# A fused two-layer MetaFormer kernel: a strip's order of work changed, GpSimd given the FFNs' last adds, and key rows kept instead of computed again

## What is computed

```
# layer 0
x = x + conv0(ln_c(x))      # ln_c: over the 96 channels of a pixel
#   conv0: q, k, v = 1x1 convolutions; windows of 8 x 8 queries against
#   12 x 12 keys (halo 2), 6 heads of 16, relative position logits, softmax, projection
t = t + ffn0(ln_t(t))       # t: the pixels as tokens of 96
# layer 1
x = x + conv1(ln_c(x))      # per quadrant of 128 x 128 and per head of 24 (4 heads):
#   4 pooled centres, sigmoid of a cosine to each pixel, the best centre alone kept,
#   values gathered into centres, spread back to the pixels, projection
t = t + ffn1(ln_t(t))
# an FFN, with q_mul = rounding to float8 (5, 2) and q_acc to float16 (5, 10)
h = relu(q_acc(q_acc(q_mul(x) @ q_mul(W1).T) + q_mul(b1)))
y = q_acc(q_acc(q_mul(h) @ q_mul(W2).T) + q_mul(b2))
```

## Time and profile before

| | us |
|---|---|
| median of 3 runs | 9565.71 (9555.72 to 9568.57) |
| profiled execution, its own time | 9573.13 |
| its span | 9571.3 |
| TensorE busy | 8344.2 (87%) |
| TensorE weight loads busy | 6638.7 (69%) |
| VectorE busy | 7322.2 (77%) |
| ScalarE busy | 4988.4 (52%) |
| GpSimd busy | 2176.8 (23%) |
| mean granted TensorE clock | 0.905 |

### The profile page before, as it was taken

How to read it: one execution, slowest core, us unless ns; L and a number is a source line. 1 busy time by engine, 2 the same in 40 slices (tenths; PEclk the granted TensorE clock), 3 DMA queues, 4 the chain that set the end, 5 groups by cost and what they waited for, 6 DMA issues and landing times.

```text
span 9571.3 us, 441216 instructions
## 1 busy us (share of the span) xinstructions
PE 8344.2 (87%) x175538; PEld 6638.7 (69%) x175538; DVE 7322.2 (77%) x24166; ACT 4988.4 (52%) x9994; POOL 2176.8 (23%) x4356
## 2 busy tenths in 40 slices
PE   8999999998888888888888888988888989888665
PEld 6777777777767767777777766776777777776443
DVE  5777777778787777787777778777778778877666
ACT  3555445445555555555555555555555555555445
POOL 2323222222222222222222222222222222222000
PEclk9999999999999999999999999999999999998555
DMA  2111112112122122222222212222222222221111
GB/s 59 49 45 46 49 49 52 50 47 60 53 58 59 53 56 59 55 58 57 55 54 59 56 51 58 58 55 54 60 55 55 60 55 54 60 55 50 57 57 61
DMA packets 191968, 525.03 MB, mean 55 GB/s; under 512 B 33372, under 2 KB 66972, under 8 KB 189980
## 3 DMA queue, kind: packets, MB, share of 16 engines
q1 hardware_dynamic: 190204, 498.89, 19.3%
HBM read 252.61 MB, written 168.30 MB: 44 GB/s over the span
## 4 chain that ended last, share of the span: by engine, by line
PE 59%; DVE 26%; issue 8%; ACT 6%; DVEq 1%; SPq 0%; ACTq 0%; DMA 0%; POOL 0%; POOLq 0%
PE scores_x L644 10%; PE flipped L666 6%; PE bank L551 5%; PE misc L560 4%; PE pv L694 3%; PE bank L614 3%; PE bank L912 3%; DVE maxes L1510 3%; PE pv L688 3%; PE scores_x L585 2%; DVE z L1625 2%; PE bank L939 2%; PE pv L895 2%; PE bank L621 2%; DVE shifted L1518 2%
## 5 line engine op out<-in xcount | busy, mean ns | idle before, releaser
L1510 DVE TENSOR_REDUCE maxes<-scores_x 128x6 f32<-128x864 f32 x1024 | 1079.1, 1054 | 1046.3 <-PE scores_x L644 973.6
L1957 POOL TENSOR_TENSOR vrest<-vstage,vmask 96x384 f32<-96x384 f32 x512 | 431.5, 843 | 5592.6 <-ACT vstage L1141 5592.6
L644 PE MATMUL scores_x<-keys,queries 64*64 64x144 f32 x24576 | 1101.4, 313 | 436.6 <-DVE shifted L1518 414.8
L644 PEld LDWEIGHTS scores_x<-keys,queries 64*64 64x64 f32 x24576 | 803.8, 144 | 678.0 <-issue 627.9
L1179 ACT ACTIVATE probs<-flipped 128x384 f32<-128x384 f32 x1024 | 497.6, 486 | 1320.1 <-PE flipped L666 1320.1
L1518 DVE TENSOR_TENSOR shifted<-scores_x,maxes 128x768 f32<-128x768 f32 x1024 | 970.2, 948 | 0.0
L606 PE MATMUL bank<-xn,wq 97*32 97x64 f32 x24576 | 869.4, 221 | 56.7 <-issue 56.0
L666 PE MATMUL flipped<-ident,shifted 128*128 128x128 f32 x6144 | 918.6, 289 | 0.1
L603 PE MATMUL bank<-xt,wq 97*32 97x64 f32 x24576 | 846.6, 221 | 65.3 <-issue 51.0
L603 PEld LDWEIGHTS bank<-xt,wq 97*32 97x32 f32 x24576 | 727.7, 110 | 248.7 <-issue 224.8
L1129 ACT ACTIVATE queries<-bank 128x512 f32<-128x512 f32 x768 | 458.6, 597 | 835.6 <-PE bank L606 835.6
(11 more groups left out here) (185 smaller groups left out, 18387.2 us busy)
## 6 DMA issues: line engine op xcount, KB each, us to landing
x_in<-x_dram SPq DMA_DIRECT2D x128, 594.0 KB
keys<-kst SPq DMA_DIRECT2D x768, 99.0 KB
xn_kept<-xn SPq DMA_DIRECT2D x128, 388.0 KB, 3.9
later<-xn_kept SPq DMA_DIRECT2D x128, 388.0 KB, 3.3
x_tok<-tok_dram SPq DMA_DIRECT2D x128, 384.0 KB, 3.5
x_kept<-x SPq DMA_DIRECT2D x128, 384.0 KB, 2.4
later<-x_kept SPq DMA_DIRECT2D x128, 384.0 KB, 3.7
out_dram<-later SPq DMA_DIRECT2D x128, 384.0 KB, 2.5
```

Source lines behind the costliest of these rows:

```text
L644: last = mm(score[e][64 * j:64 * j + 64, g * NKEY:(g + 1) * NKEY], queries[64 * e:64 * e + 64, g, w, :], keys[64 * e:64 * e + 64, g, :, WS ...
L1510: V.tensor_reduce(maxes[:, p % 2, :, :], sc, AX.X, ALU.max).then_inc(max_ready.sem, 1)
```

## The change

In short, part by part; p numbers are pairs.

1. Only the 8 new rows of a strip are loaded, normalised and turned into keys, in 3 chunks of 352 columns (means, centring, squares, variances, spreads, key matmuls); the 4 rows shared with the strip above are copied by GpSimd (`keep_halo`) inside `xn` and `kst`. Quadrants are ordered so that a column of 32 strips runs on; at its start the top rows come by DMA (`store_tops`, `load_top`), made by two more passes of the first chain in setup.
2. Values of group 0 leave the tail and take the place of group 1 in the head; group 1 comes after the scores of pair 1, in the other banks.
3. Mixing leaves the tail: matmuls at the end of TensorE's pair 5, adds at the end of VectorE's pair 5, before the maxima of pair 6.
4. The stream's statistics: `next_stats` in pair 6, `pool_stats` in pair 7.
5. Half 1 of FFN 0's statistics and normalisation: pairs 0 and 1 of the next strip, its root in one chain with layer 1's. The flip of z of that half goes to pair 2, and so does ScalarE's copy of it. The root of the features' norm shares a chain with that of x's variance.
6. `output` and `output_c` run on GpSimd. The pooling sums its four tiles on GpSimd first, so TensorE has two matmuls.
7. All three groups of variance matmuls stand in pair 3.

```diff
@@ TensorE, attend @@
-                make_values(n, 1, work)
+                make_values(n, 0, work)
                 for p in range(TILES):
                     if p + 1 < TILES:
                         scores(p + 1)
+                    if p == 0:
+                        if on.c3:
+                            pe.wait_ge(hc_evac.sem, hc_evac.at(n - 1, 6))
+                        make_values(n, 1, fill)
...
                     if p == 3 and ahead:
-                        variance(n + 1, 2, on)
-                        variance(n + 1, 3, on)
+                        for c in range(3):
+                            variance(n + 1, c, on)
...
-                    if p == 2 and ahead:
-                        if b1:
-                            pe.wait_ge(zt_ready.sem, zt_ready.at(n - 1, 2))
-                        variance(n + 1, 0, on)
-                        variance(n + 1, 1, on)
+                    if p == 2 and b1:
+                        if on.b:
+                            pe.wait_ge(ft_ready.sem, ft_ready.at(n, 2))
+                        flip_z(n - 1, 1)
...
                     if p == 5:
                         if b2:
                             pool(n - 2)
+                        if on.c1:
+                            pe.wait_ge(v_stored.sem, v_stored.at(n, 8))
+                            mix(n, 0)
+                            mix(n, 1)
...
                 weigh(TILES - 1)
-                if on.c1:
-                    for u in range(2):
-                        if ahead:
-                            pe.wait_ge(normed.sem, normed.at(n + 1, 4 - u))
-                        pe.wait_ge(v_stored.sem, v_stored.at(n, 8))
-                        mix(n, u)
...
-                    make_main(n + 1, 0, fill)
...
-                    make_rest(n + 1, 0, fill)
@@ ScalarE, attend @@
-                    store_queries(n + 1, 5)
-                    store_rest(n + 1, 0, fill)
                 if on.c2:
                     quantise_c(n, 4)
                     quantise_c(n, 5)
+                if ahead:
+                    store_queries(n + 1, 5)
@@ VectorE, attend @@
-                    if p == 0 and on.c2:
-                        stats_c(n, 1 - par)
+                    if p == 0:
+                        if on.c2:
+                            stats_c(n, 1 - par)
+                        if b1:
+                            ffn_stats(n - 1, 1)
...
-                    if p == 1 and on.c2:
-                        rsqrt_c(n)
+                    if p == 1 and b1:
+                        ffn_normalise(n - 1, 1, False, on.c2)
...
-                    if p == 2 and on.c3:
-                        output_c(n, 0, par)
-                        output_c(n, 1, par)
...
                         normalise(0)
+                        if on.c1:
+                            mix(n, 0, par)
+                            mix(n, 1, par)
                     if p == 6:
                         if b1:
-                            dve.wait_ge(xn2_ready.sem, xn2_ready.at(n - 1, 0))
-                            if on.b2:
-                                dve.wait_ge(x2_stored, n * 16 - 16)
-                            output(n - 1, 0)
-                            output(n - 1, 1)
+                            next_stats(n - 1)
...
+                        if b1:
+                            pool_stats(n - 1)
-                if on.c1:
-                    mix(n, 0, par)
-                    mix(n, 1, par)
-                if b1:
-                    next_stats(n - 1)
                 normalise(1)
                 ffn_stats(n, 0)
-                if b1:
-                    pool_stats(n - 1)
                 ffn_normalise(n, 0, b1)
...
                 residual(1)
-                ffn_stats(n, 1)
-                ffn_normalise(n, 1, False)
@@ VectorE, drain: in lengths only the clamp is left; the chain is @@
+            def lone_root(n):
+                rsqrt(rs_b_chain, n, 128, TILES * E1, newton_d, 0,
+                      [(0, TILES * E1, rs_b_chain[3][:, 0:32], newton_n)])
@@ GpSimd @@
+            def keep_halo(n):
+                pool.wait_ge(q_ready.sem, q_ready.at(n, 6))
...
+                P.tensor_copy(xn_flat[0:PROW, 0:TOP], xn_flat[0:PROW, NEW:STRIP]
+                              ).then_inc(halo_ready.sem, 1)
+                pool.wait_ge(k_loaded, n * (16 * NH) + 16 * NH)
...
+                P.tensor_copy(kst[0:C, 0:TOP], kst[0:C, NEW:STRIP]).then_inc(halo_ready.sem, 1)
+            def output(f, u):
+                pool.wait_ge(y_evac.sem, y_evac.at(f, u + 1))
+                pool.sem_inc(gate, 1)
+                P.tensor_tensor(y16[:, u, :, :], y16[:, u, :, :],
+                                b2q[0][:, None, :].to_broadcast([128, 4, C]), ALU.add
+                                ).then_inc(y_biased.sem, 1)
+                pool.wait_ge(y_biased.sem, y_biased.at(f, u + 1))
+                pool.sem_inc(gate, 1)
+                P.tensor_tensor(x2[:, 4 * u:4 * u + 4, :], x1[:, 4 * u:4 * u + 4, :],
+                                y16[:, u, :, :], ALU.add).then_inc(x2_ready.sem, 1)
...
                 mask_values(n, 0)
                 repeat_rest(n, 2)
+                if column:
+                    take_top(column)
+                elif on.ahead:
+                    keep_halo(n)
+                mask_values(n, 1)
+                repeat_rest(n, 3)
+                if on.c3:
+                    output_c(n, 0, par)
+                    output_c(n, 1, par)
                 if on.b2:
                     normalise_stream(n - 2)
-                mask_values(n, 1)
-                repeat_rest(n, 3)
                 mask_values(n, 2)
                 mask_values(n, 3)
+                if on.b1:
...
+                    output(n - 1, 0)
+                    output(n - 1, 1)
                 if on.ahead:
                     gather(n + 1)
```

398 lines of the change are left out of this document (253 added, 145 removed).

## The result

The changed kernel takes **10089.4 us** (median of 4 runs, 10055.6 to 10169.5), the kernel before 9567.1 beside it: ratio 1.0557, 95% interval 1.0490 to 1.0625. It is 5.6% slower where 4.5% faster was forecast. The profiled execution's own time is 10110.99 (span 10109.2).

The account below looks back on a forecast made before the run. No single engine bounds it; full strips decide. Full strips 94 x -4.5, second stage -72, first -9, drain +40, setup +38 sum to -426: 9147 from 9573.1, less 7.4 gives 9140 us. Its range was 9000 to 9330; 8 in 10, 8860 to 9420.

Parts of the forecast that it names:

- Pair 5's wait: Full strips: mixing's adds delay pair 6's maxima and shift, TensorE idles 2.4 us; pair 5 in all +2.75.
- It costs: First two stages: statistics queue behind GpSimd's FFN output in pair 6, 2.2 us a first-stage strip, 3.5 a second-stage one.
- 2 late: First stage: VectorE's work in pair 1 comes 2 us late, within a forecast of -0.5 a strip.
- The clock term: Full strips: the new idle time may bring 6.8 us at half clock, at a bit over one in two: +1.9 us.
- The tail: From last attended values to scores of pair 1: 13.5 us instead of 21.86, -8.3 a full strip, the largest term.
- Pair 0: Full strips: half clock behind the idle time goes, values are added, narrower chunks help: -0.3 us; +1.65 if half clock stays.
- Pairs 1 and 2: Full strips: less mean and variance work on TensorE, -0.4 and -0.65 us; VectorE up to 0.7 late from GpSimd contention.
- the third rival: VectorE's SBUF operations wait for whole new GpSimd instructions, making the kernel slower: 9700 us, chance 0.09.
- The second rival: The wait only moves: mixing costs 4, pair 1's VectorE work 1.5 late, both bring half clock; 9470 us, chance 0.11.
- Pair 3: Full strips: twelve variance matmuls stand where eight stood, +0.8 us.
- the pattern strip: The full strip used for the estimates is 0.4 us longer than the average one, which was taken off the gain.
- Drain: After the last strip: GpSimd's adds beside the root chain and the lone root's steps, about +1 for each of 36, +40 us.

Follow-up runs that it names:

- e3: The changed kernel with mixing's adds behind pair 6's shift and the stream's statistics behind x's normalisation; 9510.0 us.
- e2: The changed kernel with the stream's statistics moved from pair 6 to pair 7, behind x's normalisation; 9890.1 us.
- e12: e5 with the values of group 0 and half 1's statistics, root and z back in the tail, in the first two stages alone; 9148.4 us.
- e5: e3 with FFN 1's second bias and residual adds back on VectorE (pair 2, drain); 9230.6 us.
- e11: e5 with half 1's statistics, root and z back in VectorE's tail; 9353.4 us.
- x1: The kernel before with FFN 0's second bias and residual adds on GpSimd and nothing else; 9583.9 us against 9570.4, ratio 1.0001.
- e6: e5 with FFN 0's adds on VectorE too, in pair 6 behind mixing's adds; 9301.0 us.
- e9: e5 with the values of group 0 back in the tail and its front, group 1 at the head; 9344.0 us.
- e8: e5 with root and z of half 1 ahead of pair 1's centring, and the values of group 0 back in the tail; 9478.0 us.
- e13: e5 with the values of group 1 ahead of the scores of pair 1 instead of behind them; 9413.1 us.

## Why the prediction was wrong

**Pair 5's wait: right.** 2.52 for 2.4, in every full strip; with its half clock 3.8 (e3 against e2) for 4.3. The condition "TensorE for the shift of pair 6" was met to the word.

**A wait without its clock: the failed step for the first two stages.** "It costs" was said of GpSimd's output there, 2.2 and 3.5 a strip; the idle time was 4.1, and no clock was charged for it, nor for the "2 late" of pair 1. The clock term was taken for full strips only. Removing the wait gave 6.6 and 6.2 a strip (e2), and the whole first stage lost 10.3 where 0.5 was to be gained; the old order there gave another 3.3 (e12). The stage with the best clock had the most to lose: 0.98 in the earlier trace rows was read as a reason for a bigger gain, but a stage at full clock pays the most for a new wait. The -0.5 of the first stage does not come out of its own terms either: -3.7, +1.2, +2 and +2.2 add to +1.7, and with the second stage's -1.1 and -1.8 to -1.2.

**The tail: the failed step for the full strips.** -8.3, with -0.65 for pairs 6, 7 and keys, was forecast; measured from the scores of pair 7 to those of pair 1 is -3.9 (33.4 to 29.5). Half clock there is +3.7 us (+1.8 of time). Without the waits it is -5.4 (e5), so 3.5 are missing even then, and most of it is idle time of TensorE. The forecast let 4.43 go and put nothing in its place; in e5 the idle time of this stretch fell by 1.3 alone (6.3 to 5.0). 1.0 stayed at the scores of pair 1, between the query groups it rose by 1.2, and before the scores of pair 0 came 0.5. And VectorE bounded the tail less than I had it: its 5.5 us for half 1 were worth 1.6 to 2.0 (e11).

**Pair 0:** +0.5 for -0.3. Half clock there fell from 5.1 to 2.8 and not to nothing.

**Pairs 1 and 2: contention was there and had a place.** -1.05 was forecast, +1.6 came. I allowed 0.7 against 1.7 of slack from the earlier trace rows; in fact layer 1's adds run beside the root in 55 of 91 strips. e5 against e3 puts it at 79 us in the drain and, by the profiled executions, 2.7 a full strip, 253 of the 566 us missed there; by the medians (279 us in all) 2.1 a strip and 200. So the third rival was right on the mechanism (chance 0.09) and wrong on the reach: x1 and e6 show FFN 0's adds costing nothing by contention. Its 9700 was not the time either. The second rival had the wait behind pair 1 with its half clock (1.5 us, -1 a strip, 9470), and none charged the clock behind GpSimd's output in the first two stages.

The Trainium skill, "SBUF — State Buffer", section "Who interferes with whom", says that a VectorE instruction with two SBUF inputs, or in a two-port mode, and a GpSimd one that reads SBUF lock each other out. The rows agree: steps that read two tiles went from 0.17 to 0.77 to 0.85 beside adds of 0.91, while the maxima and the statistics (1.36 to 1.38 in all kernels) did not move. The rule does not say which of these meetings delay TensorE.

Together: a full strip came 6.0 us longer than forecast (+1.5 for -4.5). The tail gives 5.0 of it, less the 1.9 that the clock term had allowed; pairs 1 and 2 give 2.7 and pair 0 0.8; pair 3 and the 0.4 for the pattern strip take the rest off.

**Pair 3** +0.5 for +0.8, **pair 4** 0, **setup** +51 for +38, **GpSimd's adds** 0.91 for 0.84: near enough. **Drain** +94 for +40: a root step beside `output_c` costs 0.83 to 0.87 for 0.17, three or four times a drain step, from its timeline:

```profile
9701.90 0.87 DVE L1449 TENSOR_SCALAR rz<-rz 128x8 int32<-128x8 int32 x1
9702.81 0.83 DVE L1456 TENSOR_TENSOR rz<-rz 128x8 f32<-128x8 f32 x1
9703.67 0.17 DVE L1458 TENSOR_TENSOR rz<-rz 128x8 f32<-128x8 f32 x1
9703.87 0.85 DVE L1460 SCALAR_TENSOR_TENSOR rz<-rz 128x8 f32<-128x8 f32 x1
```

**Of the signs named beforehand**, those of being wrong: full strips above 71 came (73.5); the clock of 0.90 stood on its mark; root steps took 0.22 us on average and 0.29 in pair 1, just under the mark of 0.3, and GpSimd's adds 0.91, not 1.5. Of those of being right, only the waits of pair 5 and of the statistics (33 of the first 34 strips) were seen. From the last attended values to the scores of pair 1 it is 18.2 us in the mean of the full strips (22.9 before), not 13 to 14, and the first stage is not nearly as before (65.5 for 55.3). e12, with two moves on VectorE, one pair of adds taken back and the old order for two groups of work in the first two stages, takes 9148, which is the forecast of 9140. So the change held a gain behind three waits, but about half of the one worked out: the forecast's -4.5 a full strip contained 4.3 for the mixing wait and its clock, so without them it would have been -8.8, and e12 has neither and reaches -4.6. That the two times meet is luck.

**Open.** Why full strips still have about 2.3 us of half clock behind the variances with almost no idle time; no run moved them. What the halo rows that are kept, the narrower chunks and the pooling on GpSimd are worth by themselves: no run took one of them back alone. And whether the idle time between query groups can be had back in full strips: in e9 it could, but VectorE's pair 1 was in the way.

## What to carry to other kernels

When work leaves one engine's tail for its body, list for every wait that the moved instruction brings which instructions stand behind it on that engine, and put it behind what others need first: the same adds and statistics a place or two later were worth 579 us. Charge each new stop of TensorE with the half clock behind it, in every stage and most where the clock is full now (about 1.5 us of time for each us of wait, by e2 and e3). And put GpSimd's two-input work away from VectorE's short SBUF steps, or leave it on VectorE: 1.8 us of VectorE work in a slack pair cost less than 3.6 us on GpSimd beside a root.

## What the hardware showed that was not expected

**TensorE stops between the query groups with nothing to wait for.** The idle time there has almost no releaser but "issue". Page rows of the second matmul of a group, changed kernel and e9 (with two groups of longer matmuls between):

```profile
L665 PE MATMUL bank<-xn,wq 97*32 97x64 f32 x24576 | 976.0, 236 | 131.3 <-issue 130.5
```
```profile
L665 PE MATMUL bank<-xn,wq 97*32 97x64 f32 x24576 | 903.5, 224 | 67.1 <-issue 66.1
```

Gaps over 0.3 us end a median of 1.5 us (1.3 to 1.8 for eight in ten) after an instruction fetch of 16 KB has ended, by the instruction queue's packets; of the query matmuls that follow without a gap only about one in eight starts at such a distance. There were some 100 such gaps before and 195 after. A fetch took 1.08 us without data transfers and about 1.2 beside the key loads (over 1.5 in one of twenty), in the changed kernel. The gap at 5816.07 is 2.30 long:

```profile
5816.07 0.24 PE L662 MATMUL bank<-xt,wq 97*32 97x64 f32 x1 [2.30 <-issue]
```

That the fetch causes the gaps is an inference from the times and from e8 and e9; no run changed the fetch itself.

**A wait removed from TensorE comes back later and larger.** In full strips e9 took 1.6 and e13 0.8 us of idle time from TensorE's tail and head; 1.0 and 1.2 came back at the scores of pair 3 with 2.7 and 3.0 us more of half clock behind it, and both strips are longer (by 1.2 and 1.5 than e5's, by 0.9 and 1.2 than e12's, which are the same code).
